# A graph layer and an attention block on one core: the term of the zeroed rows moved from TensorE to VectorE, loads and the last layer norm reordered

## The reference, cut to what matters

```
row_zero  = x.sum(-1) == 0
q_exp     = where(row_zero[..., None], 0, cond[:, None, :])
self_feat = concat([x, q_exp]) @ W_self.T + b_self
for d in (0, 1):                    # 16 heads, the keys are the first 20 rows
    A    = adjacency (d = 0) or its transpose (d = 1), 11 labels per pair
    w    = softmax(q k / sqrt(dh), masked by A.sum(-1) > 0, + A @ w_bias + b_bias)
    out += heads of (w @ self_feat[:20]) @ Wout[d] + bout[d]
x1 = x + relu(self_feat + out)
```

```
h = gamma * ln(x1) + beta;  q, k, v = h @ Wqkv.T + bqkv       # 16 heads of 32
h1 = softmax(q k) / sqrt(512) @ v @ Wp.T + bp + x1
out = gamma * ln(h1) + beta + h1
```

## Time and profile before

| | |
|---|---|
| time, median of 3 runs | 1320.75 us (1319.14 to 1328.9) |
| the profiled execution | 1323.24 us, its span 1321.4 us |
| busy: PE, DVE, ACT, POOL | 93%, 68%, 48%, 67% of the span |
| TensorE's granted clock | mean 0.96 |
| prologue, graph to the last scores, boundary | 0 to 87 us, 87 to 445 us, 445 to 500 us |
| attention, end | 500 to 1300 us, 1300 to 1321.4 us |

### The profile page before, as it was taken

One profiled execution on the slowest core, in us unless ns is written; L12 is line 12 of the kernel. 1 busy time (PEld: TensorE's weight loads), 2 busy tenths in 40 slices (PEclk: granted clock), 3 DMA queues, 4 the chain that ended last, 5 costly groups with the idle time before them and its releaser, 6 DMA issues.

```text
span 1321.4 us, 20312 instructions
## 1 busy us (share of the span) xinstructions
PE 1225.3 (93%) x6040; PEld 831.9 (63%) x6040; DVE 893.8 (68%) x1447; ACT 637.5 (48%) x1108; POOL 881.3 (67%) x565
## 2 busy tenths in 40 slices
PE   6989799999999679899999999899999999899983
PEld 4357577777777557466666666566676576566651
DVE  2445578777877865656776776676675686676745
ACT  1323353556345435455465465465465465455552
POOL 1115467776776645665887886887887788788833
PEclk9989899999999889899999999999999999999997
DMA  9883255446444663423434434433533534524401
GB/s 335 320 306 95 65 206 211 148 161 237 179 155 157 200 185 110 130 58 102 143 83 113 141 85 113 137 89 105 145 87 103 150 79 106 146 79 107 121 25 56
DMA packets 106532, 184.07 MB, mean 139 GB/s; under 512 B 38864, under 2 KB 50448, under 8 KB 101184
## 3 DMA queue, kind: packets, MB, share of 16 engines
q1 hardware_dynamic: 94896, 150.46, 37.3%
q10 hardware_dynamic: 11536, 32.40, 7.8%
HBM read 83.92 MB, written 48.01 MB: 100 GB/s over the span
## 4 chain that ended last, share of the span: by engine, by line
PE 73%; DMA 6%; DVE 5%; issue 3%; SPq 3%; ACT 2%; POOL 2%; ACTq 1%; DVEq 0%; POOLq 0%
PE g_bank L1078 9%; PE a_bank L1785 9%; PE a_bank L1834 8%; PE a_bank L107 8%; PE a_bank L108 7%; PE a_bank L1798 7%; PE a_bank L109 7%; DMA hl<-t_rows 3%; PE g_bank L107 3%; PE g_bank L108 3%; PE g_bank L109 3%; DMA out_y<-h 2%; PE a_bank L1845 2%; SPq L1305 2%; PE g_bank L1122 1%
## 5 line engine op out<-in xcount | busy, mean ns | idle before, releaser
L1661 DVE TENSOR_REDUCE keep<-a_bank 128x1 f32<-128x512 f32 x496 | 333.4, 673 | 228.7 <-PE a_bank L1798 223.5
L1550 ACT ACTIVATE pt<-a_bank 128x512 f32<-128x512 f32 x512 | 303.4, 597 | 367.9 <-PE a_bank L1785 343.3
L1383 POOL TENSOR_TENSOR acc<-acc,pt 128x1024 f32<-128x1024 f32 x120 | 286.7, 2389 | 15.8 <-ACT pt L1550 7.7
L1785 PE MATMUL a_bank<-sq_stack,sk_stack 98*128 98x512 f32 x512 | 219.8, 429 | 6.7 <-DMA sq_stack<-sht 3.0
L1798 PE MATMUL a_bank<-sk_stack,sq_stack 96*128 96x512 f32 x496 | 201.7, 407 | 2.4 <-DVE keep L1661 2.3
L1378 POOL TENSOR_TENSOR acc<-pt 128x1024 f32<-128x1024 f32 x60 | 143.4, 2389 | 85.6 <-PE a_bank L1845 63.1
L1785 PEld LDWEIGHTS a_bank<-sq_stack,sk_stack 98*128 98x128 f32 x512 | 97.9, 191 | 95.9 <-issue 57.5
L1078 PE MATMUL g_bank<-m,sf 128*128 128x320 f32 x512 | 140.3, 432 | 1.5 <-ACT g_bank L762 1.5
L1679 DVE RECIPROCAL rden<-a_bank 128x128 f32<-128x128 f32 x128 | 120.5, 943 | 19.5 <-PE a_bank L1828 19.5
L1834 PE MATMUL a_bank<-pt,v 128*32 128x512 f32 x1024 | 128.6, 622 | 0.0
L1078 PEld LDWEIGHTS g_bank<-m,sf 128*128 128x128 f32 x512 | 96.6, 190 | 40.6 <-issue 1.9
(11 more groups left out here) (200 smaller groups left out, 2421.4 us busy)
## 6 DMA issues: line engine op xcount, KB each, us to landing
sq_stack<-qh SPq DMA_DIRECT2D x256, 64.0 KB, 2.0
sk_stack<-kh SPq DMA_DIRECT2D x256, 64.0 KB, 2.0
m<-m_rows SPq DMA_DIRECT2D x8, 1600.0 KB, 8.3
xraw<-in_x_t SPq DMA_DIRECT2D x8, 1024.0 KB, 10.7
xn<-in_x SPq DMA_DIRECT2D x8, 1024.0 KB, 5.4
h_rows<-xn ACTq DMA_DIRECT2D x8, 1024.0 KB, 4.8
t_rows<-houth SPq DMA_DIRECT2D x8, 1024.0 KB, 3.9
t_rows<-houtl SPq DMA_DIRECT2D x8, 1024.0 KB, 6.9
```

Of the source, the lines that this page charges most:

```text
L1383: nc.gpsimd.tensor_tensor(acc[:, two, :], acc[:, two, :], pt[:, step + 1, two, :], ALU.add).then_inc(s["sum_done"], 1)
L1550: nc.scalar.activation(pt[:, i, 2 * half + k, :], bank[:, k, :], ACT.Exp).then_inc(s["exp_done"], 1)
L1661: nc.vector.reduce_max(mx[:, half, k, n:n + 1], bank[:, 2 + e % 2, :], AX).then_inc(s["emax_done"], 1)
L1785: nc.tensor.matmul(bank[:, k, :], sk[c % 2][0:3 * DH + 2, j, i * P:(i + 1) * P], sq[c % 2][0:3 * DH + 2, j, :], start=True, stop=True).the ...
```

## The change

The eight parts of it, by place:

1. **Zeroed rows.** The four products of `sq` with `z` per batch go. In the prologue `ccol` (the same product as columns, 4x8 of 128) comes from 16 products of 128x8. ScalarE computes `added` = `nz` * `ccol` + bias from SBUF (`condition`), and VectorE adds it to each bank as it evicts it (`self_features`). TensorE waits for `nz` ahead of the fourth bank.
2. **Labels.** In a step, VectorE sums the labels' weights behind the attention of b-1 instead of at the end of the step before, and counts them behind the statistics of the residual, where GpSimd takes the power. GpSimd's `label_products` and ScalarE's `labels_float` move in the same way, and the labels' load can go earlier.
3. **Columns.** The eight loads of `gcol` and `bcol` stand behind the load of `m` at the end of step 1.
4. **Boundary.** The split of `wvl` is done by GpSimd ahead of `add_bp`; `split_lo(1)` by VectorE between residual and the norm's last step; `store_h(B-2)` stands behind the weights' splits; the shift rows come two slots earlier.
5. **Loads of h.** The second half of `hh` and `hl` is issued by SP in group 1, between the stacks of q and the store of the output.
6. **Last layer norm.** (h-mean)*gamma on VectorE, h+beta on GpSimd beside it, then one operation with rstd on VectorE; nothing on ScalarE. The reciprocals are computed one tile ahead of the quotients.
7. **Prologue.** Loads in the order x, first and second half of `W_self`; the rest follows part 1.
8. Buffers: `z`, `hot`, `hot20`, `sq` and `cond64` go; `spare` holds `added`.

The diff, cut to its core:

```diff
 def self_features(b):                                   # TensorE, graph
-    out, col = bank[:, SFB[o], :], slice(o * P, (o + 1) * P)
+    col = slice(o * P, (o + 1) * P)
+    if o == FC - 1:
+        pe.wait_ge(s["nz_done"], b + 1)
     for f in range(FC):
-        mm3(nc, out, t["w1h"][:, f, col], t["w1l"][:, f, col], xh[:, f, :], xl[:, f, :], f == 0, False)
-    if o == FC - 2:
-        pe.wait_ge(s["z_done"], b + 1)
-    for k in {FC - 2: range(FC - 1), FC - 1: (FC - 1,)}.get(o, ()):
-        nc.tensor.matmul(bank[:, SFB[k], :], t["sq"][:, k * P:(k + 1) * P], z[:, :],
-                         start=False, stop=True).then_inc(s["sf_ready"], 1)
+        last = mm3(nc, bank[:, SFB[o], :], t["w1h"][:, f, col], t["w1l"][:, f, col], xh[:, f, :], xl[:, f, :],
+                   f == 0, f == FC - 1)
+    last.then_inc(s["sf_ready"], 1)
...
-def self_features(b, par):                              # ScalarE, graph
+def condition(b):
+    act.wait_ge(s["sf_done"], 4 * b)
+    act.wait_ge(s["nz_done"], b + 1)
...
-        act.wait_ge(s["sf_ready"], 4 * b + o + 1)
-        nc.scalar.activation(sf2[:, par, o, :], bank[:, SFB[o], :], ACT.Identity, bias=t["bself"][:, o:o + 1])
+        nc.scalar.activation(added[:, o, :], nz[:, :], ACT.Identity, bias=t["bself"][:, o:o + 1],
+                             scale=t["ccol"][:, o, ds(b, 1)]).then_inc(s["added"], 1)
...
+def self_features(b, par):                              # VectorE, graph
+    dve.wait_ge(s["att_done"], 4 * b - 4 if not isinstance(b, int) else max(4 * b - 4, 0))
+    for o in range(FC):
+        dve.wait_ge(s["sf_ready"], 4 * b + o + 1)
+        dve.wait_ge(s["added"], 4 * b + o + 1)
+        nc.vector.tensor_tensor(sf2[:, par, o, :], bank[:, SFB[o], :], added[:, o, :], ALU.add).then_inc(s["sf_done"], 1)
...
 def step(b, par, last):                                 # VectorE, graph
     attention(b - 1, 1 - par)
-    if not last:
-        label_count(b + 1)
-    else:
-        split_lo(1)
+    labels(b)
     softmax(b, True, not last)
     if not last:
-        labels(b + 1)
+        self_features(b + 1, 1 - par)
...
 def step(b, par, last):                                 # SP, graph
     if not last:
         sp.wait_ge(s["xl_done"], 4 * b + 4)
         load_first(b + 1)
-        sp.wait_ge(s["adj_step"], 5 * b + 5)
+        sp.wait_ge(s["adj_step"], 5 * b + 1)
+        sp.wait_ge(s["adjf_done"], b + 1)
         load_adj(b + 1)
...
         load_m(b + 1)
+    if isinstance(b, int) and b == 1:
+        load_columns()
     if isinstance(b, int) and b < 3:
         load_w(b - 1)
...
         if last:                                        # GpSimd, graph, softmax
+            split_lo(2)
             for i in range(NT):
                 add_bp(b - 1, i)
...
     if c < 2 or more:                                   # SP, attention, group c
         stacks(*ahead(b, c, 2), 0, (0,))
+    if c == 1 and more:
+        load_t(b + 1)
     if c == 1 and later:
         store_y(b - 1, 0)
...
-if slot == 14 and c == 1 and more:                      # ScalarE, attention
-    load_t(b + 1, (1,))
...
-hy = last_tiles()                                       # GpSimd, end
-for i in range(NT + 2):
-    if i < NT:
-        rsqrt(B - 1, i)
-    if i >= 2:
-        y = hy[i - 2][0]
-        pool.wait_ge(s["ln_done"], 4 * (B - 1) + i - 1)
-        nc.gpsimd.tensor_tensor(y, y, rows[:, 1, :], ALU.add).then_inc(s["addb_done"], 1)
+for i, (y, _, hb) in enumerate(last_tiles()):
+    n = 4 * (B - 1) + i + 1
+    pool.wait_ge(s["h1_done"], n)
+    nc.gpsimd.tensor_tensor(hb, y, rows[:, 1, :], ALU.add).then_inc(s["addb_done"], 1)
+    pool.wait_ge(s["ve_done"], n)
+    nc.gpsimd.tensor_tensor(rstd[:, i % 2:i % 2 + 1], ve[:, i % 2:i % 2 + 1], mhalf, ALU.pow).then_inc(s["rstd_done"], 1)
...
-    nc.vector.tensor_tensor(y, y, ti, ALU.add).then_inc(s["y_done"], 1)        # VectorE, end
+    nc.vector.scalar_tensor_tensor(y, ti, rstd[:, (i - 1) % 2:(i - 1) % 2 + 1], hb,
+                                   ALU.mult, ALU.add).then_inc(s["y_done"], 1)
```

279 lines of the change are left out of this document (141 added, 138 removed).

## The result

The changed kernel takes 1351.87 us (median of 4 runs, 1350.79 to 1354.94), the kernel before 1324.83 us beside it: ratio 1.0218, 95% interval 1.0175 to 1.0262. It is 2.2% slower. I had forecast 1307 us, a range up to 1322 us, and a chance of 0.07 for slower. The profiled execution of the changed kernel has a span of 1349.9 us, that of before 1321.4 us.

What follows compares the result with a forecast made beforehand. TensorE, by what it executes or waits for, was taken as the bound. Terms of −1.5 up to the attention, −8 for loads of h and −5 at the end gave −14.5 us; forecast 1307 us, range 1290 to 1322.

Steps and rivals of the forecast that it cites:

- Products of the zeroed rows: Graph steps: four products fewer, VectorE's evictions costing nothing; −0.9 us each in steps 3 to 7, −1.6 in step 0.
- the scores wait for VectorE's evictions: Rival for the graph steps: scores start 1 us or more late per step, +5 us, 1312 us; chance 0.08.
- Step 1: Graph step 1: with column loads and labels out of the way, −7.1 us beyond step 0, products included.
- Step 2: Graph step 2: the moved column loads delay `xraw`, a 5.6 us stall and half clock, +7.6 us; bounds −0.9 and +8.5.
- Boundary: Graph to attention: the last residual waits for x's reload, so 6.1 us gained earlier become −1.5; bounds −10 and +5.
- Loads of h: Attention block: the wait moves from slot 18 to slot 16, shrinking from 2.6 to about 1.5 us; −8, bounds −24 and +10.
- clean rival: Attention block: SP takes the second half cleanly, wait under 1 us, clock holds; −21 instead of −8, about 1294 us; chance 0.18.
- slower rival: Attention block: stacks and shift row wait behind the half on SP's queue, 7 us a batch, +22, 1336 us; chance 0.07.
- End: Last layer norm: 3.3 us per tile on VectorE, four tiles 13.2 us; −5 us (−4 to −6.5).
- Prologue: Before step 0: sixteen small products replace eight, beside loads that must land anyway; gain 0.5 us, between −2 and +2.

Runs made afterwards that it cites:

- e2: The changed kernel with the store of x issued behind the four additions and the labels' conversion on ScalarE: 1331.72 us, ratio 1.0063.
- e9: The kernel of e8 with the labels of batch 1 left whole in step 1: 1308.62 us, ratio 0.9888.
- e6: The kernel of e2 with the eight loads of columns in step 1 between the load of `xraw` and that of the labels: 1320.88 us, ratio 0.9974.
- e1: The changed kernel with the labels back at their old place on every engine, their sums ahead of the evictions: 1338.55 us, ratio 1.0106.
- e5: The kernel of e2 with the eight loads of columns ahead of step 1 again: 1327.66 us, ratio 1.0022.
- e12: The kernel before with the last layer norm's part and the column loads in step 1 between `xraw` and the labels' load: 1314.16 us, ratio 0.9936.
- e10: The kernel of e9 with GpSimd adding `bp` before it splits `wvl`, and x stored after the second of four weight splits: 1304.61 us, ratio 0.9823.
- e8: The kernel of e6 with the labels' work cut in two, between the evictions and behind the attention products: 1322.0 us, ratio 0.9973.
- e11: The kernel of e10 with the second half of h on ScalarE's queue in slot 12, ahead of `load_h`: 1310.63 us, ratio 0.9891.
- e7: The kernel before with part 5 alone, the second half of h on SP's queue: 1323.59 us, ratio 0.9995.
- e14: The kernel of e10 with the second half of h on SP's queue behind the stacks of k and the shift row: 1288.45 us, ratio 0.9749.
- e15: The kernel before with only the second half of h on SP's queue, behind the stacks of k and the shift row: 1308.86 us, ratio 0.9909.

## Why the prediction was wrong

*Products of the zeroed rows.* This step failed. It said that the evictions' place on VectorE costs nothing because the labels that stood there took as long, and took −0.9 us for each of steps 3 to 7; the traces show +16.7 us in steps 3 to 6 where it had −3.6. I counted VectorE's time and not its waits: the evictions wait for ScalarE's additions, and the fourth of those stood behind `store_h`, which waits for GpSimd. Moving that store gave 3.1 us a step (e2), half of it waits and most of the rest the clock that fell behind them. I wrote down the change of `condition` and named the store in front of it, but never asked who waits for the instruction behind it. The second half of the failure is that I let the labels move "at nothing": 4.9 us where there was room for 3.6 puts the residual 1.2 us later, and against e9, which cuts them in two, it is 1.5 us a step (44.75 us in e2 and e6, 43.2 in e9). With both mended the step is 43.2 us, close to the −0.9 of the forecast. The rival "the scores wait for VectorE's evictions" named the engine, at 5 us where these steps lost 16.7; the wait that it names, 1.4 us a step, shows only in e1.

*Step 1.* Right, −7.8 for −7.1. The sum left open which of two causes it was, and they don't add: the labels alone moved give nothing beyond the products (e5, 49.3 us), the columns alone at most 1 us (e12), both together 7.

*Step 2.* The mechanism was right and the size too small: +11.9 for +7.6. The columns' own share is 11.1 us by e6 against e2, where I had taken 8.5. TensorE waited 9.5 us (2.6 and 6.8) where I had taken 5.6. The store's stall adds nothing here: without it (e2) the step is as long, 56.1 us.

*Boundary.* The mechanism was right: the wait for `kl` went (one of 3.4 us for GpSimd's part of the softmax stands near it now), TensorE waited 7.7 us for the residual, where I had it 10 us early, and storing x earlier took 7 us back (e10). Of the +9.1 us the labels' place has 3.5 to 7: with the labels cut in two this stretch is 135.7 (e9) and 132.1 us (e8), without it 139.1 (e6), and it was 132.1 before.

*Loads of h.* The step failed in its size. The wait moved from slot 18 to slot 16 as forecast, by the two ways that were named (the store and `load_h`; the shift row), but it is 3.2 us on average instead of 1.5. That was the upper end of what I gave. What makes the small transfers late is 1 MB issued ahead of them, on SP's queue or on the other (e11). The store's landing was right (8.25 us for some 8.5), but it is issued a microsecond later, behind the two issues of the half, and behind it stand `load_h`, an exponential and only then TensorE's product, 1.2 us more that I had left out. So −8 became between 0 (e7) and +4. The clean rival didn't come true. The slower rival named the place at 7 us a batch, and the first groups show 5.1; it put it down to the order on SP's queue, and e11 shows the same lateness without that order.

*End.* Right, though the table's −3.2 for −5 (−4 to −6.5) doesn't look it. Four tiles take the 13.2 us that were reckoned. In seven other profiles with part 6 this stretch is 6.1 us shorter than before; in the one of the changed kernel the clock fell to 0.50 for 6.8 us ahead of the first sum, and that took 3 us back.

*Prologue.* +0.7 against −0.5; step 0 starts between 86.3 and 89.9 us in the profiles of all these kernels, so nothing can be said of it.

The total: the forecast of −14.5 became +28.5 us in the spans. 20.3 of the difference of 43.0 stand in steps 3 to 6, 10.2 in the attention block, 5.4 at step 7 and the boundary, 4.3 in step 2. Some of it is the clock: over the whole span it cost the changed kernel's profile up to 13.4 us more than that of before.

## The version that beats both

e14 has all parts of the change, with five of its places mended: the store of x behind the additions, the columns behind `xraw`, the labels cut in two, x stored before `wvl` is split, and the second half of h behind the stacks. It takes 1288.45 us, 2.5% less than the kernel before and by the two ratios 4.6% less than the change as it was.

## What to carry to other kernels

When work moves from a busy engine to one with room, look at what each moved instruction waits for and follow that back through the producer's queue: a DMA issue that waits on a third engine, harmless where nothing stood behind it, cost 3 us a step here. A large load is issued after the small transfers that the next product needs: issued before them it delayed them from its own queue and from another. And a slow group of issues goes where its queue is idle. Where several parts are changed at once, price each by itself: here the load of h alone was worth nothing as written (e7) and 12 us once mended (e15), and the last layer norm 6 us where the clock held. A difference of 3 us in one stretch of one profile can be the clock alone: look at the granted clock there before looking for another cause.

## What was not expected

- A wait of TensorE of 1.3 to 2.0 us left the clock at 1.00 four times in e14, while waits of 1.8 and 1.9 us in the kernel before were followed by 0.50. In steps 2 to 6 of the changed kernel TensorE waits 1.8 to 1.9 us for the residual each time, and the clock fell behind three of these waits and held behind two. What makes the difference isn't settled.
- The last operation on the labels (128x160, two inputs from SBUF) took 0.39 us in the kernel before, where GpSimd was idle beside it, and 1.28 us in the changed one (the row at 345.99), where GpSimd was splitting low parts. In all eight batches before it took 0.38 to 0.39 us, and in the changed kernel 1.27 or 1.28 in the six in which it ran beside GpSimd, 0.38 in the other two. This alone is 0.9 of the 4.9 us. The Trainium skill (GPSIMD Engine Reference, Specifications) has the two share an interface to SBUF in that case; the rows agree. `blocked`, with one input, went from 0.23 to 1.3 us beside GpSimd in both kernels.
